# Five-stage language-model tower on one core: split float32 state-space products, expert blocks with the tokens as stationary operand, and register loads one pair ahead

## The chip, the cores and the metric

The kernel runs on one core of one Trainium2 chip. The time is what the device reports for one execution of the whole program, in microseconds (us). The median of three runs of the kernel before is 3116.32 us (3112.61 to 3125.64).

## The reference, cut to what matters

Eight sequences of 512 tokens, 256 channels each (x is 4096 x 256 in float32), pass through five stages, one after the other:

- **Tower**, four layers: `x = x + ssm(layernorm(x))`, then `x = x + gelu(layernorm(x) @ w1 + b1) @ w2 + b2`.
- Window attention, a stage that the change doesn't touch.
- **bfloat16 experts**: 8 experts, each token goes to its 2 best.
- Relative attention, not touched.
- **float32 experts**: 16 experts, the 2 best, beside a shared path.

The two formulas on which the change works:

```
# state-space part of a tower layer, for every sequence; H is a scan over the 512 tokens
u = x @ B                    # 256 -> 64 states
h = sigmoid(A) * h + u       # one step a token
y = H @ C + x @ D            # 64 -> 256 and 256 -> 256

# bfloat16 expert e, on the tokens that chose it
p1  = x @ mlp1[e].T + bias1[e]            # 256 -> 512, gate and linear part interleaved
act = g * sigmoid(1.702 g) * (lin + 1)    # g = min(p1 even, 7), lin = clip(p1 odd)
p2  = act @ mlp2[e].T + bias2[e]          # 256 -> 256
```

## The kernel before

All of x lies in SBUF from start to end. Each engine has a program of its own, written out by hand, and semaphores tie them together; there is no scheduler. A stage ends when all its engines have passed its last barrier.

**Tower (`tower_stage`).** 32 steps, one for a layer and a sequence. On TensorE, step j (`step`, L576) is: the first MLP product of sequence j, channels tile by tile (`mlp_in`, L557, in three parts of 4, 2 and 2 tiles); between these parts the two state-space products of the *next* step, `ssm_in(j + 1)` (L533) and `ssm_out(j + 1)` (L543 for D, L544 for C); the transposes of the normalised rows for the step after next (`turn1`, L132); the second MLP product (`mlp_out`, L571, four token tiles) with the transposes of the next step (`turn2`) between the second and the third tile. The MLP products take float32 data in two parts of type fp32r, a rounded high part and the rest, and sum three products, high x high, high x low and low x high (`TERMS`, L547); ScalarE makes the high part, VectorE the low one. The state-space products take plain float32; the profile shows two MATMUL rows for one such product, and one for a product in fp32r. ScalarE's step (L395) is 16 Gelu passes, `turn(j + 2)` (L371: two copies out of PSUM) and `turn2(j + 1)` (four copies, high and full). VectorE's step (L476) is, in this order: `norm1(j + 2)`, `low_hid` 0, `scan(j + 1)` (L430), `low_hid` 2 and 4, `add_y(j + 1)`, statistics of the second norm, `low_hid` 6, its application, `add_o` first half (L454), `low_xn2T(j + 1)` (L468), `add_o` second half. In the first step of a layer VectorE and ScalarE first split w2, in the last one they split the next w1. GpSimd gathers the embedding rows at the start (L172, 32 gathers), and computes the reciprocal roots.

**bfloat16 experts (`bf16_experts_stage`).** First, for each sequence b: norm, a second (mean square) norm, routing, and a scatter of the rows to DRAM, sorted by expert (8 indirect DMAs a sequence, L1172, from GpSimd). GpSimd's loop is, for b = 0 to 7: root of the first norm of b (`pool_rstd`, L117), root of the mean square of b (L1178), scatter of b - 2. VectorE can centre sequence b only when L117 is done. After the routing SyncE stores eight pad blocks (L1118), each at a row that it reads into a register, and only then loads blocks. Then 36 pairs of blocks of 128 rows go through a pipeline; in its iteration i TensorE does the transposes of pair i (L1495), the first product of pair i - 1 (L1508, with the bias L1509) and the second of pair i - 3 (L1520, L1523). The first product has the *weights* as stationary operand, 128 columns of them at an offset from a register, and 128 tokens as moving operand, 24 matrix instructions a pair; its result has the hidden channels on partitions, as the second product wants it. ScalarE's iteration is: copy of the transposes of i (L1243), Gelu of i - 1 (L1250), high part of i - 1 (L1257), copy of the result of i - 4 (L1264):

```
                    act.wait_ge(act_ready, j + 1)
                    if j >= 2:
                        act.wait_ge(y_done, j - 1)
                    act.activation(act_s[:, j % 2, 0, :, :, :], act_b[:, j % 2, :, :, :], ACT.Identity).then_inc(high_ready, 1)
```

Here j is i - 1, so that this copy waits until TensorE has finished the second product of pair i - 3, and the copy of the result of pair i - 4 stands behind it. GpSimd sends that result to DRAM with two indirect DMAs (L1186), and SyncE loads pair j into a ring of six buffers when pair j - 6 has been sent (L1127, L1128).

**float32 experts (`experts_stage`).** 39 pairs in a pipeline of the same kind: transposes of i (L2428), gate and up product of i - 1 (L2438), transposes of i - 2 (L2447), down product of i - 3 (L2455). The expert's offset is read into registers of TensorE between the transposes of i and the product of i - 1:

```
                    offset[j] = [pe.value_load(owner_at[0:1, 2 * j + s:2 * j + s + 1], min_val=0, max_val=(EX - 1) * WROW) for s in range(2)]
```

The bfloat16 stage has the same loads behind the first product, one pair ahead (`find`, L1481).

## Time and profile before

| | |
|---|---|
| runs, median (lowest to highest) | 3116.32 us (3112.61 to 3125.64) |
| profiled execution, its own time | 3127.48 us |
| its span, first to last instruction | 3125.8 us |
| TensorE busy, share of the span | 2495.2 us, 80% |
| VectorE busy | 1474.5 us, 47% |
| ScalarE busy | 1263.8 us, 40% |
| GpSimd busy | 691.0 us, 22% |
| mean granted TensorE clock | 0.845 of 2.4 GHz |

A busy time is the union of an engine's instructions, so that two that overlap count once. The granted clock is what the throttle gave TensorE: 1.00 stands for 2.4 GHz and 0.50 for 1.2 GHz. The profiled execution is 11.2 us above the median of the runs. By stage, roughly: the tower to 1190 us, window attention to 1423 us, the bfloat16 experts to 1937 us (preparation to 1590 us, the pairs to 1896 us), relative attention to about 2700 us, the float32 experts to the end (the pairs from 2905 to 3080 us).

### The profile page before, as it was taken

What the parts mean: (1) busy time and instruction counts of PE and PEld (TensorE: products, weight loads), DVE (VectorE), ACT (ScalarE), POOL (GpSimd) and SP (SyncE); (2) the same over time, 40 slices, a digit from 0 to 9 for tenths busy, and PEclk for the clock granted to TensorE, in tenths of its full rate; (3) what the DMA queues carried; (4) which work ended last, traced back from release to release, by engine and by line L of the source; (5) the groups of instructions that cost most, each with busy time, mean ns of one, the idle gap of its engine ahead of it and who ended that gap; (6) DMA issues with size and microseconds to landing.
All of it is one profiled execution on the core that took longest, in us unless ns stands there. A gap on an engine that the chain in (4) does not pass through costs nothing. (4 is left out here: it accounts for less than half of the span.)

```text
span 3125.8 us, 44495 instructions
## 1 busy us (share of the span) xinstructions
PE 2495.2 (80%) x13409; PEld 1759.7 (56%) x13409; DVE 1474.5 (47%) x4318; ACT 1263.8 (40%) x2520; POOL 691.0 (22%) x824
## 2 busy tenths in 40 slices
PE   2999999999999996982169991588988888695883
PEld 1777777777777774762135551255555555472662
DVE  3544554444454435634522225366666666460224
ACT  1434443444344432432312223376667667410221
POOL 4111111111111103203622222111121112226332
PEclk7999999999999998985555555699999999767987
DMA  9300100000000001222111114122222112222336
GB/s 217 41 1 5 30 1 0 13 23 1 5 3 1 0 1 36 41 49 62 39 44 49 48 49 140 47 67 65 63 62 63 59 41 66 55 62 90 102 118 217
DMA packets 202515, 162.18 MB, mean 52 GB/s; under 512 B 104945, under 2 KB 160673, under 8 KB 202337
## 3 DMA queue, kind: packets, MB, share of 16 engines
q1 hardware_dynamic: 184258, 118.51, 14.2%
q0 software_dynamic: 13856, 37.30, 4.0%
q10 hardware_dynamic: 4224, 4.19, 0.4%
q8 instruction: 88, 1.44, 0.2%
q14 instruction: 89, 0.73, 0.1%
HBM read 89.99 MB, written 69.95 MB: 51 GB/s over the span
## 5 line engine op out<-in xcount | busy, mean ns | idle before, releaser
L571 PE MATMUL psum_o<-w_s,hid_s 128*128 128x256 f32 x3072 | 384.2, 284 | 19.0 <-ACT hid L404 19.0
L557 PE MATMUL psum_h<-xn2T_s,w_s 128*128 128x512 f32 x1536 | 388.7, 402 | 5.4 <-ACT hid L404 3.3
L571 PEld LDWEIGHTS psum_o<-w_s,hid_s 128*128 128x128 f32 x3072 | 371.9, 188 | 26.9 <-issue 19.0
L403 ACT ACTIVATE hid_s<-psum_h,b 128x512 fp32r<-128x512 f32 x256 | 176.0, 688 | 435.1 <-PE psum_h L557 418.8
L557 PEld LDWEIGHTS psum_h<-xn2T_s,w_s 128*128 128x128 f32 x1536 | 277.3, 188 | 114.8 <-ACT hid L404 46.7
L1848 DVE CUSTOM_DVE_ANT_0 ra_z<-ra_psum_s,ra_rhat 128x128 f32<-128x128 f32 (+3 forms) x512 | 225.7, 482 | 230.5 <-PE ra_psum_s L1947 217.4
L1789 ACT ACTIVATE ra_p<-ra_z,ra_nm 128x128 f32<-128x128 f32 (+3 forms) x512 | 244.4, 555 | 0.0
L1959 PE MATMUL ra_psum_p<-ident,ra_p 128*128 128x128 f32 x1280 | 190.2, 302 | 62.5 <-POOL ra_p L1714 62.5
L1959 PEld LDWEIGHTS ra_psum_p<-ident,ra_p 128*128 128x128 f32 x1280 | 155.7, 153 | 98.0 <-issue 75.9
L1714 POOL TENSOR_SCALAR_AFFINE_SELECT ra_p<-ra_p 128x512 f32<-128x512 f32 x128 | 81.2, 634 | 556.4 <-DVE ra_p L1876 556.4
L1781 ACT ACTIVATE ra_pt<-ra_psum_p 128x1024 f32<-128x1024 f32 x128 | 131.0, 1024 | 166.5 <-PE ra_psum_p L1959 166.5
L473 DVE TENSOR_TENSOR hid_s<-hid,hid_s 128x1024 fp32r<-128x1024 f32 x128 | 155.5, 1215 | 84.3 <-ACT hid L404 84.0
L404 ACT ACTIVATE hid<-psum_h,b 128x512 f32<-128x512 f32 x256 | 174.0, 680 | 0.0
L1971 PE MATMUL ra_psum_o<-ra_pt,ra_v_now 128*32 128x512 f32 (+3 forms) x1024 | 171.5, 481 | 0.8 <-ACT ra_pt L1783 0.8
L1876 DVE TENSOR_SCALAR ra_p<-ra_p,ra_em 128x128 f32<-128x128 f32 (+3 forms) x512 | 162.6, 380 | 1.4 <-issue 1.4
L117 POOL TENSOR_TENSOR ln2n_rstd<-ln2n_var_eps,minus_half 128x4 f32<-128x4 f32 x32 | 32.3, 1008 | 525.7 <-DVE ln2n_var_eps L113 525.7
L543 PE MATMUL psum_y<-wd,xn1T 128*128 128x256 f32 x512 | 144.4, 405 | 2.0 <-DVE state L430 1.9
L1393 DVE TENSOR_SCALAR be_lin<-be_bank 128x512 f32<-128x512 f32 x36 | 24.9, 692 | 244.4 <-PE be_bank L1509 244.4
L379 ACT ACTIVATE xn2T_s<-psum_t,ln 128x512 fp32r<-128x512 f32 x64 | 46.4, 775 | 211.6 <-PE psum_t L132 211.6
L1947 PE MATMUL ra_psum_s<-ra_k_st,ra_q_st 48*128 48x128 f32 (+3 forms) x512 | 118.6, 352 | 15.0 <-DMA ra_k_st<-ra_scratch 14.5
L1186 POOL DMA_INDIRECT be_results<-be_ys,be_zs x72 | 69.0, 959 | 248.4 <-ACT be_ys L1264 236.5
L454 DVE TENSOR_TENSOR x<-psum_o,x 128x512 f32<-128x512 f32 (+1 forms) x64 | 44.3, 691 | 167.6 <-PE psum_o L571 167.6
(354 smaller groups left out, 4359.2 us busy)
## 6 DMA issues: line engine op xcount, KB each, us to landing
ex_slots<-blank SPq DMA_DIRECT2D x1, 10296.0 KB, 68.4
ex_zT<-ex_slots SPq DMA_DIRECT2D x39, 264.0 KB
ex_rows<-ex_slots SPq DMA_DIRECT2D x8, 1056.0 KB, 9.8
w<-in_L_tok_w SPq DMA_DIRECT2D x8, 1024.0 KB
be_rows<-be_results SPq DMA_DIRECT2D x8, 1024.0 KB, 5.3
ra_scratch<-ra_hi SPq DMA_DIRECT2D x32, 256.0 KB
ra_scratch<-ra_lo SPq DMA_DIRECT2D x32, 256.0 KB
ra_q_st<-ra_scratch SPq DMA_DIRECT2D x128, 64.0 KB, 1.8
```

The lines of the kernel that those rows point to most:

```text
L403: act.activation(hid_s[:, 0, m, :], psum_h[:, m % 2, :], ACT.Gelu, bias=b1[:, m:m + 1])
L404: act.activation(hid[:, m, :], psum_h[:, m % 2, :], ACT.Gelu, bias=b1[:, m:m + 1]).then_inc(hid_ready, 1)
L473: dve.tensor_tensor(hid_s[:, 1, m:m + 2, :], hid[:, m:m + 2, :], hid_s[:, 0, m:m + 2, :].bitcast(F32), ALU.subtract).then_inc(hid_lo, 1)
L543: pe.matmul(out, xn1T[:, parity, k, tok], wd[:, k, :], start=(k == 0), stop=False)
L557: mm = pe.matmul(psum_h[:, m % 2, :], w1_s[:, w_part, k, m * P:(m + 1) * P], xn2T_s[:, x_part, k, :], start=(n == 0 and k == 0), stop=(n = ...
L571: mm = pe.matmul(psum_o[:, t // 2, (t % 2) * D:(t % 2 + 1) * D], hid_s[:, h_part, m, t * P:(t + 1) * P], w2_s[:, w_part, m, :], start=(n = ...
L1781: act.activation(out[:, 0:8, :], psum_p[:, 0:2, :].rearrange("p c (a b) -> p (c a) b", a=4), ACT.Identity).then_inc(pt_act, 1)
L1789: act.activation(p[:, i % 2, t, 0:n], z[:, i % 2, t, 0:n], ACT.Exp, scale=SCALE, bias=nm[:, i % 2, t:t + 1]).then_inc(exp_done, 1)
L1848: dve.tensor_tensor_reduce(out=z[:, i % 2, t, 0:n], in0=scores[t], in1=rhat[:, i * T + T - n:(i + 1) * T], scale=1.0, scalar=0.0, op0=ALU. ...
L1876: last = dve.tensor_scalar(pt_, pt_, em[:, (i - 1) % 2, t:t + 1], None, ALU.max)
L1959: mm = pe.transpose(psum_p[:, c, a * P:(a + 1) * P], p[:, i % 2, q, k * P:(k + 1) * P], S.ident[:, :])
L1971: mm = pe.matmul(psum_o[u * HC:(u + 1) * HC, k * P:T], v_now[:, slot, k, :], pt[:, slot, first:first + n, :].rearrange("p a b -> p (a b)") ...
```

## The change

Tower: B, C and D are held in one tile `ssm` and split into two fp32r parts, as w1 and w2 are (`high_ssm` on ScalarE, `low_ssm` on VectorE, 1024 columns, once a layer, in the last step of the layer before). B is loaded twice side by side, and C twice, one copy below the other, so that the state appears on 128 partitions, twice the same 64 states. The normalised rows are split too: `turn` makes four copies in place of two, and `low_xn1T` is a new pass on VectorE, behind the application of the second norm. After the scan VectorE rounds the 128 rows of the state, and subtracts on the lower 64 rows, so that one product with K = 128 gives the high and the low part of the state times the high part of C, and a product with K = 64 adds the high part times the low part of C.

bfloat16 experts: the tokens become the stationary operand and 512 columns of weights the moving one, 6 matrix instructions a pair in place of 24; Gelu and clip run in two halves each, and the result is turned round with four float32 transposes into a PSUM bank, from which the high and the low part are made, one iteration later than before. The transposes of the rows have one PSUM buffer in place of two. GpSimd computes the root of the first norm one sequence ahead.

float32 experts: the register loads go behind the product, one pair ahead.

The diff, cut to its core:

```diff
-        wb = sb("wb", [P, DK, NS])
-        wc = sb("wc", [NS, D])
-        wd = sb("wd", [P, DK, D])
+        NP = 2 * NS
+        SSM_B, SSM_C, SSM_D = 0, DK * NP, DK * NP + D
+        SSM = SSM_D + DK * D
+        ssm, ssm_s = sb("ssm", [P, SSM]), sb("ssm_s", [P, 2, SSM], F32R)
...
-                (state_ready, NB * l, b_loaded, [(wb[:, :, :], mat("L0_tok_B")), (decay[:, :], decay_all[:, ds(l, 1)])]),
-                (y_done, NB * l, cd_loaded, [(wc[:, :], A["L0_tok_C"][ds(l, 1), :, :].rearrange("o s d -> (o s) d")),
-                                             (wd[:, :, :], mat("L0_tok_D"))]),
+                (ssm_split, l, ssm_loaded, ssm_pairs(l)),
+                (state_ready, NB * l, step_loaded, [(decay[:, :], decay_all[:, ds(l, 1)])]),
...
-                for k in range(DK):
-                    act.activation(xn1T[:, parity, k, :], psum_t[:, k, :], ACT.Identity,
-                                   scale=ln1[:, 0, k:k + 1], bias=ln1[:, 1, k:k + 1]).then_inc(xn1T_ready, 1)
+                if later(j):
+                    act.wait_ge(xn1T_lo, j)
+                for out, count in ((xn1T_s[:, parity, 0, :, :], 0), (xn1T[:, :, :], 1)):
+                    for k in range(DK):
+                        ins = act.activation(out[:, k, :], psum_t[:, k, :], ACT.Identity, scale=ln1[:, 0, k:k + 1], bias=ln1[:, 1, k:k + 1])
+                        if count:
+                            ins.then_inc(xn1T_ready, 1)
...
-                dve.tensor_tensor_scan(state[:, :], decay[:, 0:1].to_broadcast([NS, T]), psum_y[0:NS, 0, :],
+                dve.tensor_tensor_scan(state[:, :], decay[:, 0:1].to_broadcast([NP, T]), psum_y[0:NP, 0, :],
                                        0.0, ALU.mult, ALU.add).then_inc(state_ready, 1)
+                dve.wait_ge(state_ready, j + 1)
+                dve.tensor_copy(state_s[:, :], state[:, :]).then_inc(state_hi, 1)
+                dve.wait_ge(state_hi, j + 1)
+                dve.tensor_tensor(state_s[NS:NP, :], state[NS:NP, :], state_s[NS:NP, :].bitcast(F32), ALU.subtract).then_inc(state_split, 1)
...
+            def low_xn1T(j, parity):
+                dve.wait_ge(xn1T_ready, DK * (j + 1))
+                dve.tensor_tensor(xn1T_s[:, parity, 1, :, :], xn1T[:, :, :], xn1T_s[:, parity, 0, :, :].bitcast(F32),
+                                  ALU.subtract).then_inc(xn1T_lo, 1)
...
                     norm2_apply(j + 1)
-                if w1_of is not None:
-                    low_w1(w1_of)
+                if more2:
+                    low_xn1T(j + 2, parity)
+                if next_of is not None:
+                    low_w1(next_of)
...
-                for k in range(DK):
-                    mm = pe.matmul(psum_y[0:NS, 0, :], wb[:, k, :], xn1T[:, parity, k, :], start=(k == 0), stop=(k == DK - 1))
+                for n, (x_part, w_part) in enumerate(TERMS):
+                    for k in range(DK):
+                        mm = pe.matmul(psum_y[0:NP, 0, :], ssm_s[:, w_part, SSM_B + k * NP:SSM_B + (k + 1) * NP], xn1T_s[:, parity, x_part, k, :],
+                                       start=(n == 0 and k == 0), stop=(n == 2 and k == DK - 1))
...
-                    for k in range(DK):
-                        pe.matmul(out, xn1T[:, parity, k, tok], wd[:, k, :], start=(k == 0), stop=False)
-                    mm = pe.matmul(out, state[:, tok], wc[:, :], start=False, stop=True)
+                    for n, (x_part, w_part) in enumerate(TERMS):
+                        for k in range(DK):
+                            pe.matmul(out, xn1T_s[:, parity, x_part, k, tok], ssm_s[:, w_part, SSM_D + k * D:SSM_D + (k + 1) * D],
+                                      start=(n == 0 and k == 0), stop=False)
+                    if t == 0:
+                        pe.wait_ge(state_split, j + 1)
+                    pe.matmul(out, state_s[:, tok], ssm_s[:, 0, SSM_C:SSM_D], start=False, stop=False)
+                    mm = pe.matmul(out, state_s[0:NS, tok], ssm_s[0:NS, 1, SSM_C:SSM_D], start=False, stop=True)
...
+            nm[0].pool_rstd(pool, S.minus_half, 0)
             for b in range(NB):
-                nm[b % 2].pool_rstd(pool, S.minus_half, b // 2)
+                if b + 1 < NB:
+                    nm[(b + 1) % 2].pool_rstd(pool, S.minus_half, (b + 1) // 2)
...
-                    act.activation(gate[:, j % 2, :, :, :].rearrange("p s t n -> p (s t n)"), bank[2 + 2 * (j % 2)][:, :],
-                                   ACT.Gelu_apprx_sigmoid).then_inc(gated, 1)
-                if 0 <= i - 1 < PAIRS:
-                    j = i - 1
-                    act.wait_ge(act_ready, j + 1)
+                    for s in range(2):
+                        if s:
+                            act.wait_ge(lin_ready, 2 * j + 1)
+                        act.activation(gate[:, j % 2, s, :], bank[1 + 2 * (j % 2) + s][:, 0:I], ACT.Gelu_apprx_sigmoid).then_inc(gated, 1)
+                if 0 <= i - 2 < PAIRS:
+                    j = i - 2
+                    act.wait_ge(a_turned, j + 1)
                     if j >= 2:
                         act.wait_ge(y_done, j - 1)
-                    act.activation(act_s[:, j % 2, 0, :, :, :], act_b[:, j % 2, :, :, :], ACT.Identity).then_inc(high_ready, 1)
+                    act.activation(act_s[:, j % 2, 0, :], psum_a[:, :], ACT.Identity).then_inc(high_ready, 1)
...
                     for s in range(2):
-                        for it in range(IK):
-                            for half in range(2):
-                                to = bank[2 + 2 * (j % 2) + half][:, (s * IK + it) * P:(s * IK + it + 1) * P]
-                                at = (it * 2 + half) * P
-                                for k in range(DK):
-                                    pe.matmul(to, w1T[:, k, ds(offset[j][s] + at, P)], zsT[:, j % 2, s, k, :], start=(k == 0), stop=False)
-                                mm = pe.matmul(to, b1_row[0:2, ds(offset[j][s] + at, P)], ones2[0:2, :], start=False, stop=True)
+                        to = bank[1 + 2 * (j % 2) + s]
+                        for k in range(DK):
+                            pe.matmul(to[:, :], zsT[:, j % 2, s, k, :], w1T[:, k, ds(offset[j][s], WSTEP)], start=(k == 0), stop=False)
+                        mm = pe.matmul(to[:, :], ones2[:, :], b1_row[0:2, ds(offset[j][s], WSTEP)], start=False, stop=True)
                     mm.then_inc(p1_done, 1)
...
+                if 0 <= i - 2 < PAIRS:
+                    j = i - 2
+                    pe.wait_ge(act_ready, j + 1)
+                    if j:
+                        pe.wait_ge(low_ready, j)
+                    for s in range(2):
+                        for it in range(IK):
+                            at = (s * IK + it) * P
+                            mm = pe.transpose(psum_a[:, at:at + P], act_b[:, j % 2, s, it * P:(it + 1) * P], S.ident[:, :])
+                    mm.then_inc(a_turned, 1)
...
+            find(0)
             for i in range(PAIRS + 3):
...
-                    offset[j] = [pe.value_load(owner_at[0:1, 2 * j + s:2 * j + s + 1], min_val=0, max_val=(EX - 1) * WROW) for s in range(2)]
...
                     mm.then_inc(bgu_done, 1)
+                    if j + 1 < PAIRS:
+                        find(j + 1)
```

## Rows read from the trace of the kernel before

**Rows 1.** Windows: busy us (x instructions) of PE, PEld, DVE, ACT, POOL; clock, DMA.

```profile
80.00:1160.00 1080.00, 1055.86 (x5858) 823.21 (x5856) 524.16 (x1113) 461.73 (x703) 137.39 (x92) 1.00 0.05 9
...
1590.00:1896.00 306.00, 274.79 (x1368) 153.55 (x1368) 71.54 (x108) 82.61 (x145) 69.00 (x72) 0.50 0.16 48
...
2905.00:3080.00 175.00, 149.77 (x700) 121.12 (x701) 42.17 (x77) 49.38 (x117) 69.40 (x73) 0.90 0.36 108
```

**Rows 2.** Timeline, one tower step: start us, duration, engine, line.

```profile
660.65 5.99 PE L571 MATMUL psum_o<-w_s,hid_s 128*128 128x256 f32 x48
...
663.87 1.23 DVE L468 TENSOR_TENSOR xn2T_s<-xn2T,xn2T_s 128x1024 fp32r<-128x1024 f32 x1 [3.12 <-ACT xn2T L379]
...
666.48 5.99 PE L557 MATMUL psum_h<-xn2T_s,w_s 128*128 128x512 f32 x24
...
672.39 1.93 PE L533 MATMUL psum_y<-xn1T,wb 128*64 128x512 f32 x4
...
674.51 1.21 DVE L430 TENSOR_TENSOR_SCAN state<-decay,psum_y 64x512 f32<-64x512 f32 x1 [1.13 <-PE psum_y L533]
...
677.16 1.03 PE L543 MATMUL psum_y<-wd,xn1T 128*128 128x256 f32 x4
...
683.81 3.06 PE L557 MATMUL psum_h<-xn2T_s,w_s 128*128 128x512 f32 x12
...
688.06 1.45 ACT L371 ACTIVATE xn1T<-psum_t,ln 128x512 f32<-128x512 f32 x2
```

**Rows 3.** Timeline, PE alone: the start of the tower step after that.

```profile
700.78 5.98 PE L557 MATMUL psum_h<-xn2T_s,w_s 128*128 128x512 f32 x24
```

**Rows 4.** Timeline, the first step of a layer: its start and its scan.

```profile
354.30 2.95 PE L557 MATMUL psum_h<-xn2T_s,w_s 128*128 128x512 f32 x12
...
364.44 1.21 DVE L430 TENSOR_TENSOR_SCAN state<-decay,psum_y 64x512 f32<-64x512 f32 x1
```

**Rows 5.** Timeline, start of the tower: an embedding add, transposes at the low clock.

```profile
54.78 1.23 DVE L197 TENSOR_TENSOR x<-x,pos 128x1024 f32<-128x1024 f32 x1 [5.39 <-DMA x<-in_L_tok_emb,idx]
...
62.20 1.97 PE L132 MATMUL psum_t<-ident,xn 128*128 128x128 f32 x8 [19.39 <-DVE xn L123]
```

**Rows 6.** Timeline, POOL alone, bfloat16 experts, one sequence of the preparation.

```profile
1510.66 1.04 POOL L117 TENSOR_TENSOR be_n_rstd<-be_n_var_eps,minus_half 128x4 f32<-128x4 f32 x1
1515.20 1.01 POOL L1178 TENSOR_TENSOR be_rms<-be_ms_eps,minus_half 128x4 f32<-128x4 f32 x1 [3.50 <-DVE be_ms_eps L1297]
...
1526.50 1.04 POOL L117 TENSOR_TENSOR be_n_rstd<-be_n_var_eps,minus_half 128x4 f32<-128x4 f32 x1
```

**Rows 7.** Timeline, SP's queue, bfloat16 experts: the pad blocks.

```profile
1563.59 22.27 SPq L1118 DMA_DIRECT2D be_slots<-be_pads  x8
```

**Rows 8.** Timeline, bfloat16 experts, two iterations of the pairs.

```profile
1643.05 0.61 PE L1495 MATMUL be_bank<-be_ident,be_zs 128*128 128x128 bf16 x4 [1.32 <-DMA be_zs<-be_slots]
...
1647.66 0.42 PE L1520 MATMUL be_bank<-be_b_row,be_ones 1*128 x1
...
1650.57 0.60 PE L1495 MATMUL be_bank<-be_ident,be_zs 128*128 128x128 bf16 x4
1650.80 0.63 ACT L1257 ACTIVATE be_act_s<-be_w_raw 128x512 fp32r<-128x512 f32 x1 [2.30 <-PE be_bank L1523]
...
1651.34 0.58 ACT L1264 ACTIVATE be_ys<-be_bank 128x512 f32<-128x512 f32 x1
...
1659.85 0.61 PE L1495 MATMUL be_bank<-be_ident,be_zs 128*128 128x128 bf16 x4 [1.48 <-DMA be_zs<-be_slots]
```

**Rows 9.** Timeline, float32 experts: an iteration after a DMA wait, and the next.

```profile
2998.86 0.66 PE L2428 MATMUL ex_bank<-ident,ex_zT 128*128 128x128 f32 x4 [1.30 <-DMA ex_zT<-ex_slots]
...
3000.40 3.51 PE L2438 MATMUL ex_bank<-ex_w,ex_zT 128*128 x8 [0.89 <-ACT ex_zT L2173]
...
3005.27 1.89 PE L2438 MATMUL ex_bank<-ex_w,ex_zT 128*128 x8
```

**Rows 10.** Waits, same pairs: us in total, times, longest us.

```profile
PE ex_bank L2438 <- ACT ex_zT L2173: 11.4, 13, 1.0
```

More of the change, by code:

```diff
@@ L274, in mat, with ssm_pairs @@
                 return A[name][ds(l, 1), :, :].rearrange("o (k p) n -> p (o k) n", p=P)
+            def ssm_pairs(l):
+                b_twice = ssm[:, SSM_B:SSM_C].rearrange("p (k u n) -> p k u n", k=DK, u=2)
+                return ([(b_twice[:, :, u, :], mat("L0_tok_B")) for u in range(2)]
+                        + [(ssm[u * NS:(u + 1) * NS, SSM_C:SSM_D], A["L0_tok_C"][ds(l, 1), :, :].rearrange("o s d -> (o s) d")) for u in range(2)]
+                        + [(ssm[:, SSM_D:SSM].rearrange("p (k n) -> p k n", k=DK), mat("L0_tok_D"))])
             return [
@@ L297, in layer @@
                 step(l * NB + NB - 2, 0, True, not last)
-                step(l * NB + NB - 1, 1, not last, not last, w1_of=None if last else l + 1)
+                step(l * NB + NB - 1, 1, not last, not last, next_of=None if last else l + 1)
             layer(0, False)
@@ L308, in _ @@
         def _(sp):
-            sp.dma_start(decay_in[:, :], A["L0_tok_A_diag"].rearrange("l s -> s l")).then_inc(decay_loaded, 16)
+            for u in range(2):
+                sp.dma_start(decay_in[u * NS:(u + 1) * NS, :], A["L0_tok_A_diag"].rearrange("l s -> s l")).then_inc(decay_loaded, 16)
             embedding.sync_loads(sp)
@@ L312, in _ @@
             w1_first, w2_first = first[0], first[1]
-            ln1_first, b_first, cd_first, ln2_first, b1_first, b2_first = first[2:]
+            ln1_first, ssm_first, step_first, ln2_first, b1_first, b2_first = first[2:]
             sp.wait_ge(decay_ready, 1)
-            for _, _, arrived, pairs in [ln1_first, b_first, cd_first, ln2_first, w1_first, b1_first, w2_first, b2_first]:
+            for _, _, arrived, pairs in [ln1_first, ssm_first, step_first, ln2_first, w1_first, b1_first, w2_first, b2_first]:
                 for to, frm in pairs:
@@ L381, in turn2, with high_ssm @@
                             ins.then_inc(xn2T_ready, 1)
+            def high_ssm(l):
+                act.wait_ge(ssm_loaded, 80 * (l + 1))
+                if later(l):
+                    act.wait_ge(y_done, NB * l)
+                act.activation(ssm_s[:, 0, :], ssm[:, :], ACT.Identity).then_inc(ssm_hi, 1)
             def high_w1(l):
@@ L406, in step @@
                     turn(j + 2, parity)
-                if w1_of is not None:
-                    high_w1(w1_of)
+                if next_of is not None:
+                    high_w1(next_of)
                 if more:
                     turn2(j + 1)
+            high_ssm(0)
             high_w1(0)
@@ L474, in low_hid, with step @@
                                   ALU.subtract).then_inc(hid_lo, 1)
-            def step(j, parity, more, more2, w2_of=None, w1_of=None):
+            def step(j, parity, more, more2, w2_of=None, next_of=None):
                 if w2_of is not None:
                     low_w2(w2_of)
+                if next_of is not None:
+                    low_ssm(next_of)
                 if more2:
@@ L505, in _ @@
             embedding.vector_embed(dve, 1)
+            low_ssm(0)
+            low_xn1T(0, 0)
             scan(0)
@@ L514, in _ @@
             norm1(1)
+            low_xn1T(1, 1)
             for b in range(NB - 2, NB):
@@ L574, in mlp_out, with step @@
                     mm.then_inc(o_done, 1)
-            def step(j, parity, more, more2, w2_of=None, w1_of=None):
+            def step(j, parity, more, more2, w2_of=None, next_of=None):
                 mlp_in(j, range(FM // 2))
@@ L1048, in bf16_experts_stage @@
         zsT = sb("zsT", [P, 2, 2, DK, P], BF16)
-        lin = sb("lin", [P, 2, 2, IK, P])
+        lin = sb("lin", [P, 2, 2, I])
         early = w1_raw[:, :, :].rearrange("p r h -> p (r h)").bitcast(F32)
-        gate, act_b = (early[:, n * 4 * IK * P:(n + 1) * 4 * IK * P].rearrange("p (u s t n) -> p u s t n", u=2, s=2, t=IK) for n in range(2))
-        act_s = sb("act_s", [P, 2, 2, 2, IK, P], F32R)
-        square = lin[:, :, :, :, :].rearrange("p u s t n -> p (u s t n)").rearrange("p (t n) -> p t n", t=TT)
+        gate, act_b = (early[:, n * 4 * I:(n + 1) * 4 * I].rearrange("p (u s n) -> p u s n", u=2, s=2) for n in range(2))
+        act_s = sb("act_s", [P, 2, 2, T], F32R)
+        square = lin[:, :, :, :].rearrange("p u s n -> p (u s) n")
         ys = sb("ys", [P, YRING, 2, D])
@@ L2420, in _, with find @@
             offset = {}
+            def find(j):
+                offset[j] = [pe.value_load(owner_at[0:1, 2 * j + s:2 * j + s + 1], min_val=0, max_val=(EX - 1) * WROW) for s in range(2)]
+            find(0)
             for i in range(PAIRS + 3):
```

81 lines of the change are left out of this document (42 added, 39 removed).

## The prediction

> **What bounds the kernel now.** I read the windows by stage first, then the timeline inside each stage that the change touches. In the tower TensorE is busy 1056 of 1080 us at a granted clock of 1.00 [rows 1]: matrix work bounds it, and the other engines are half idle. The timeline of a step shows the same, one product against the next, with a period of 700.78 - 666.48 = 34.3 us [rows 2, 3]. In the bfloat16 pairs TensorE is busy 275 of 306 us, at 0.50 of the clock [rows 1], but two iterations of them begin with a DMA wait, and what they wait for is a ring: load, three iterations, copy of the result, scatter, next load [rows 8]. In the float32 pairs the same holds in every third iteration or so [rows 9]. In the preparation of the bfloat16 experts GpSimd's order of work sets the pace, at 1526.50 - 1510.66 = 15.8 us a sequence [rows 6].
>
> **Tower, the products.** A product of 512 columns in fp32r costs 3.06 / 12 = 0.255 us, one of 256 columns 5.99 / 48 = 0.125 us [rows 2]. `ssm_in` goes from 1.9 us (four rows of plain float32, two for each product) to 6 x 0.255 = 1.5. `ssm_out` takes 683.81 - 677.16 = 6.65 us now; it becomes 4 tiles x 8 products x 0.125 = 4.0. That is 0.4 + 2.65 = 3.05 us a step, all of it on TensorE's path.
>
> **Tower, what is added.** ScalarE's `turn` grows by 1.45 us, the price of its present two copies [rows 2]. It runs under `mlp_out` 0 and 1, which last 6 us and must have its result at their end; it would be done some 3 us earlier. The cost is nothing; without that cover it would be 1.45 us a step. `low_xn1T` is a pass like L468, 1.23 us [rows 2], behind the norm and before `add_o`, where VectorE waits for TensorE: nothing. The weights' split is once a layer about 1 us on ScalarE and 1.23 on VectorE, in the last step, where the scan waited 1.13 us for TensorE [rows 2] and the next wait has slack: nothing. The five loads on SyncE's queue in place of three or four come a step and more ahead.
>
> The serial part is the state. The scan now has two passes behind it, a rounding and a subtraction, before the C products of the first tile. The trace shows no such rounding. Its bounds are 0.4 (a third of a 1024-column pass) and 1.23 us [rows 2]; I take 0.7 for each of the two, nearest to half of the 1024 columns plus a fixed part. The scan starts at 674.51, 0.35 earlier afterwards, and ends 1.21 later; with two hand-overs the split is there at 677.0. TensorE reaches `ssm_out` at 676.8 and has six D products (0.75 us) that don't need it: it wants the split at 677.5. So the new wait is hidden by half a microsecond. At 1.23 us each it would come 0.5 us late, 16 us in 31 steps. What is queued behind these passes on VectorE are `low_hid` 2 and 4, whose Gelus come later anyway.
>
> In the first step of a layer VectorE has split w2 before, and the scan comes 364.44 - 354.30 = 10.1 us into the step, against 8.0 in the other [rows 2, 4]. There the split comes about 1.3 us late: 4 x 1.3 = 5 us. At the start of the program the longer chain (two more copies, two more VectorE passes) lies under the embedding gathers, which VectorE still awaits at 54.78 [rows 5]; but in step 0 `low_xn1T(1)` stands ahead of the last embeddings, and I give that step no gain. Tower: 30 x 3.05 - 5 = **-87 us**.
>
> **Preparation of the bfloat16 experts.** GpSimd's cycle is root (1.04), 3.50 us idle until the mean square is there, root (1.01), then eight scatters to 1526.50 [rows 6]. The idle time exists because VectorE centres a sequence only after the first root. With the root a sequence ahead, the centring falls under the scatters and the idle time goes; it stands in five of the eight cycles, so 17 us. What ends next are the scatters themselves, 10 us a sequence. The pad blocks on SyncE's queue (22.27 us, [rows 7]) hang on the last routing and move with it: **-17 us**, between -5 (the routing chain takes the idle time) and -18.
>
> **bfloat16 pairs.** An iteration of TensorE is 1650.57 - 1643.05 = 7.52 us: 4.61 for the transposes and the first product, 2.91 for the second [rows 8]. The copy of the result starts 0.77 us after that, because ScalarE's high copy waits for the second product (2.30 us idle, L1257) and the result stands behind it. From this copy at 1651.34 it is 8.51 us to the transposes of the pair two iterations later, at 1659.85 [rows 8]. Two iterations are thus 7.52 + 0.77 + 8.51 = 16.8 us, 8.4 a pair: the ring is the bound, not TensorE alone.
>
> Afterwards, at 1.2 GHz, the first product is six instructions of 512 columns, 0.43 us each (512 / 1.2 GHz; above, twice the 0.255 of [rows 2], 0.51). With 0.4 for the transposes of the rows, 4 x 1.97 / 8 = 1.0 for the new float32 transposes [rows 5] and 2.9 for the second product that makes 6.9 us (up to 7.4). The ring changes too. The high copy is an iteration later and no longer waits for the second product, so the result is copied about 4.8 us into the iteration rather than 8.3; two iterations need 4.8 + 8.51 = 13.3, 6.7 a pair. TensorE's 6.9 becomes the bound, the ring close behind. 36 x (8.4 - 6.9) = **-54 us**; at 7.4, -36. That the rows' transposes share one PSUM buffer costs nothing, as their copy is done during the second product. ScalarE has about 2.8 us of copies in 6.9.
>
> **float32 pairs.** After a DMA wait the product stands 0.89 us behind the transposes, while the registers load (the row puts it down to the copy of the transposes, which that product doesn't need) [rows 9]; 13 such waits make 11.4 us [rows 10]. Then the eight matrix instructions take 3.51 us instead of 1.89 [rows 9], as the clock has fallen in the gap. With the loads ahead the gap goes, as it did in the bfloat16 stage. It lies on the ring, so its time is won, unless the load is merely awaited longer. I take the 11 us and a third of the lost clock: **-15 us**, between 0 and -25.
>
> **The sum.** 87 + 17 + 54 + 15 = 173 us. The profiled execution took 3127.5 us, so 2954; the median of the runs is 11 us lower, and I give **2942 us** against 3116.
>
> **The rivals.**
>
> *The ring does not shorten.* If the copy of the result still comes late in the iteration, two iterations need 16 us, and the pairs win 12 rather than 54; if the float32 gap too is only exchanged for a longer DMA wait, another 12 go. About 2990 us. For it: both rings wait for DMA now. Against it: the present lateness has its cause in the row of L1257. Chance 0.14.
>
> *The products are not cheaper*: the shapes with the state behave otherwise than the MLP's, say half the gain is gone. 2985 us, chance 0.04.
>
> *Slower than before.* The place is the wait on `state_split` in `ssm_out`: if it lets TensorE stand for 2 us a step, the clock falls as in [rows 9], and the following products run at half speed. A step's 31 us of products would become some 57. It decides from 173 / 26 = 7 such steps; with 10 of them, 2942 + 260 = 3200 us. Against it: clock 1.00 over 1080 us [rows 1], no such gap in a step [rows 2], and even the dear bound makes a wait of 0.5 us. Chance 0.01.
>
> **How the numbers follow.** The forecast has 0.55, the clock 0.25, the ring 0.14, the products 0.04, slower 0.01, anything near no change 0.01. About 0.5% can be told from no change in this kernel. The forecast's own bounds are the dear state passes (+16), 7.4 us a pair (+18), the preparation (+12) and the float32 pairs (+15 or -10); not all together. The range of 2890 to 2990 us takes in the clock case and most of the ring case. Faster 0.98, same 0.01, slower 0.01.
>
> **What would show it.** Right: a tower period of 31.2 us, `ssm_out` at 4.0; 12.3 us a sequence in the preparation; 6.9 us a pair with ScalarE's L1264 before the second product's end; no wait between L2428 and L2438. Wrong: a wait of PE for DVE's state passes in every step; a clock well over 0.50 in the pairs; SyncE waiting for scatters with pairs of 8 us; a step period that stays at 33 or 34 us.

## The result, and the profile after it

The changed kernel takes 3009.68 us (median; 2993.97 to 3018.84) beside 3119.11 us for the kernel of before on the same chip: 0.964 of its time, 95% interval 0.960 to 0.969. Faster, as forecast, but by 109 us where 174 were forecast, and above the range of 2890 to 2990 us.

The stages follow one another, so each one's length can be read from the last VectorE instruction of each. All times in us; the chip of the second pair is another one, where both kernels run some 25 us or more faster:

| stage | before | after | difference | forecast | second pair |
|---|---|---|---|---|---|
| tower | 1173.8 | 1124.8 | -49.0 | -87 | 1173.2, 1121.7 |
| window attention | 249.2 | 251.8 | +2.6 | 0 | 248.6, 250.8 |
| bfloat16 experts | 512.7 | 443.4 | -69.3 | -71 | 507.5, 434.6 |
| relative attention | 784.4 | 803.9 | +19.5 | 0 | 780.4, 800.7 |
| float32 experts | 405.8 | 392.5 | -13.3 | -15 | 375.4, 361.6 |
| span | 3125.8 | 3016.2 | -109.6 | -173 | 3085.1, 2969.5 |

So two of three changed stages came out within 2 us, the tower gave 38 us less than forecast, and a stage whose code is the same in both kernels lost 20. A difference of a stage between two executions is not all due to an edit: the bfloat16 experts of the changed kernel took 443.4 and 434.6 us here, and 428.3 and 422.7 in two kernels below whose edits touch neither their preparation nor their pairs. In windows, the profile after, with the columns of [rows 1] (tower; preparation and pairs of the bfloat16 experts; relative attention; pairs of the float32 experts):

```profile
80.00:1110.00 1030.00, 1001.35 (x6182) 867.06 (x6181) 612.79 (x1211) 508.94 (x769) 158.47 (x92) 0.99 0.05 10
...
1376.00:1528.00 152.00, 23.12 (x243) 18.76 (x244) 77.64 (x382) 44.11 (x110) 92.42 (x100) 0.51 0.19 60
1528.00:1756.00 228.00, 198.22 (x782) 101.20 (x796) 74.16 (x135) 81.99 (x168) 59.45 (x62) 0.69 0.19 57
1820.00:2624.00 804.00, 646.11 (x3584) 399.85 (x3584) 483.14 (x1972) 503.60 (x1060) 150.13 (x315) 0.87 0.18 54
...
2818.00:2962.00 144.00, 126.24 (x659) 102.81 (x659) 38.83 (x71) 47.00 (x111) 65.38 (x68) 0.99 0.42 127
```

The tower is as dense as before. In the bfloat16 pairs the clock is no longer 0.50 but 0.69 on average. Relative attention had the same 3584 matrix instructions in the kernel before:

```profile
1936.00:2720.00 784.00, 630.87 (x3584) 393.53 (x3584) 484.22 (x1972) 502.22 (x1060) 149.69 (x315) 0.89 0.19 56
```

The timeline of one tower step after the change, as [rows 2]:

```profile
642.75 1.23 DVE L503 TENSOR_TENSOR xn2T_s<-xn2T,xn2T_s 128x1024 fp32r<-128x1024 f32 x1 [3.12 <-ACT xn2T L392]
...
645.36 5.97 PE L605 MATMUL psum_h<-xn2T_s,w_s 128*128 128x512 f32 x24
...
651.16 1.56 PE L578 MATMUL psum_y<-xn1T_s,ssm_s 128*128 128x512 f32 x6
...
652.91 1.22 DVE L452 TENSOR_TENSOR_SCAN state<-decay,psum_y 128x512 f32<-128x512 f32 x1 [0.65 <-PE psum_y L578]
...
654.16 0.43 DVE L455 CAST state_s<-state 128x512 fp32r<-128x512 f32 x1
654.62 0.69 DVE L457 TENSOR_TENSOR state_s<-state,state_s 64x512 fp32r<-64x512 f32 x1
...
655.36 0.88 PE L589 MATMUL psum_y<-ssm_s,xn1T_s 128*128 128x256 f32 x6
...
656.08 0.28 PE L593 MATMUL psum_y<-ssm_s,state_s 128*128 128x256 f32 x1
656.29 0.18 PEld L594 LDWEIGHTS psum_y<-ssm_s,state_s 64*128 64x128 f32 x1
656.29 0.38 PE L594 MATMUL psum_y<-ssm_s,state_s 64*128 64x256 f32 x1
656.60 0.77 PEld L589 LDWEIGHTS psum_y<-ssm_s,xn1T_s 128*128 128x128 f32 x6
...
660.60 3.06 PE L605 MATMUL psum_h<-xn2T_s,w_s 128*128 128x512 f32 x12
```

The state is split at 655.3, and TensorE needs it at 656.08: it doesn't wait. The period, from L503 to L503 of the next step, is 674.85 - 642.75 = 32.1 us (median of all steps 32.2, before 34.3); 31.2 was forecast. `ssm_out` lasts 660.60 - 655.36 = 5.24 us, not 4.0. Look at the last product of an output tile, L594: its weight load (engine PEld, which brings the stationary operand into the array) starts at the same moment as its matrix instruction, while the load of L593 starts 0.12 us ahead of its own. A tile thus costs 656.60 - 655.36 = 1.24 us, and 1.33 where such a product stands ahead of it too, and not eight times 0.125.

### The profile page after: what moved, and what is told of

Its sections match the earlier page's. It is cut to its first block and busy times, and to the rows that moved or that the text cites. A ratio compares the mean times of both kernels' runs of the same rounds, so it can differ in the third digit from the quotient of the medians.

```text
span 3016.2 us, 43729 instructions
## 1 busy us (share of the span) xinstructions
PE 2376.3 (79%) x13211; PEld 1756.8 (58%) x13225; DVE 1572.0 (52%) x4454; ACT 1319.7 (44%) x2624; POOL 716.0 (24%) x824
## 5 line engine op out<-in xcount | busy, mean ns | idle before, releaser
L605 PEld LDWEIGHTS psum_h<-xn2T_s,w_s 128*128 128x128 f32 x1536 | 284.6, 191 | 90.4 <-ACT hid L425 21.5
L2028 PE MATMUL ra_psum_o<-ra_pt,ra_v_now 128*32 128x512 f32 (+3 forms) x1024 | 182.5, 505 | 0.8 <-ACT ra_pt L1840 0.8
L2028 PEld LDWEIGHTS ra_psum_o<-ra_pt,ra_v_now 128*32 128x32 f32 x1024 | 59.9, 123 | 121.3 <-issue 108.6
L589 PE MATMUL psum_y<-ssm_s,xn1T_s 128*128 128x256 f32 x768 | 124.8, 299 | 3.0 <-DVE state L452 3.0
L1444 DVE TENSOR_SCALAR be_lin<-be_bank 128x256 f32<-128x256 f32 x72 | 30.3, 425 | 174.9 <-PE be_bank L1555 162.7
L345 POOL TENSOR_TENSOR x<-x,b 128x1024 f32 (+1 forms) x32 | 99.0, 3093 | 79.5 <-DVE xn L123 68.7
```

Of the source, the lines that this page charges most:

```text
L589: pe.matmul(out, xn1T_s[:, parity, x_part, k, tok], ssm_s[:, w_part, SSM_D + k * D:SSM_D + (k + 1) * D], start=(n == 0 and k == 0), stop=F ...
L605: mm = pe.matmul(psum_h[:, m % 2, :], w1_s[:, w_part, k, m * P:(m + 1) * P], xn2T_s[:, x_part, k, :], start=(n == 0 and k == 0), stop=(n = ...
L2028: mm = pe.matmul(psum_o[u * HC:(u + 1) * HC, k * P:T], v_now[:, slot, k, :], pt[:, slot, first:first + n, :].rearrange("p a b -> p (a b)") ...
```

## The experiments

Each kernel below is compared with runs of the kernel before on its own chip (medians 3091 to 3096 us; 3128 for the two parts undone).

**The same two kernels again.** No edit.

> The kernel of before, unchanged. Question: is the relative attention stage (identical code in both kernels; 784.4 us before at a granted clock of 0.93 in its middle, 803.9 us after at 0.89) longer in the changed kernel because of the change, or does it vary from one execution to the next? If it varies: anything between 784 and 805 us here, and the float32 experts' preparation (185.1 us before, 194.0 after) varies too. If the stage's length belongs to the kernel: 784 us within 1, and 185 us.

> The changed kernel, unchanged. If the length of the relative attention stage varies by execution: somewhere between 784 and 805 us. If it belongs to the kernel (for instance by where the stage's instructions lie): 804 us within 1. The tower's period stays at 32.2 us and the stall of 4.8 us in front of the first product of layer 2 stands again if it is a stall of the program's, not of one execution.

Measured: 780.4 and 800.7 us in relative attention. Both are 3 to 4 us below the lengths that were asked for, but the difference of 20 us is there again: it belongs to the kernel, though the stage's code is the same. The float32 preparation took 163.9 and 163.8 us here, against 185.1 and 194.0 in the first pair, so its difference of 9 us there does not come from the change. The stall ahead of the first product of layer 2, which the waits put down to "issue", is 3.1 us here, 4.8 in the first profile of the changed kernel and 1.8 in that of before.

**All 128 rows of the split state.**

```diff
-                    mm = pe.matmul(out, state_s[0:NS, tok], ssm_s[0:NS, 1, SSM_C:SSM_D], start=False, stop=True)
+                    mm = pe.matmul(out, state_s[:, tok], ssm_s[:, 1, SSM_C:SSM_D], start=False, stop=True)
```

> The changed kernel with the low part of C multiplied with all 128 rows of the split state (high and low) rather than with its upper 64. The sum gains the term low x low, which the other products leave out; the number of instructions stays. Theory: a product with 64 rows between products with 128 shows its weight load in the open, once going in and once coming out, and that is the 0.33 us by which an output tile (1.33 us) is dearer than eight products of 0.125. Then a tile takes 1.00 us, the step 32.2 - 1.3 = 30.9 us, the tower 40 us less, the kernel about 2970 us. Rival: the two products with the state cost more whatever their rows (their operand comes from VectorE's tile): the tile stays at 1.33 us and nothing changes.

Measured: 2916.73 us, 0.944 of the kernel before (0.941 to 0.947); tower 1075.4 us after 1121.7; step 30.7 us. Beside the one run of the changed kernel on this chip (2972.08 us) that is 55 us less; the tower's 46 are the edit's, the rest lies in the bfloat16 experts and in relative attention, 6 us each, where nothing was edited. The timeline of a tile in this kernel:

```profile
660.80 0.88 PE L589 MATMUL psum_y<-ssm_s,xn1T_s 128*128 128x256 f32 x6
661.41 0.19 PEld L593 LDWEIGHTS psum_y<-ssm_s,state_s 128*128 128x128 f32 x1
661.52 0.28 PE L593 MATMUL psum_y<-ssm_s,state_s 128*128 128x256 f32 x1
661.53 0.19 PEld L594 LDWEIGHTS psum_y<-ssm_s,state_s 128*128 128x128 f32 x1
661.64 0.28 PE L594 MATMUL psum_y<-ssm_s,state_s 128*128 128x256 f32 x1
...
661.76 0.40 PE L605 MATMUL psum_h<-xn2T_s,w_s 128*128 128x512 f32 x1
```

Every load is again 0.11 us ahead of its product, and the tile takes 661.76 - 660.80 = 0.96 us. The array has more work, and the product is cheaper: its number of rows, not its operand, made the difference. The profile of before shows the same mark, in its timeline of a tile:

```profile
678.12 0.29 PEld L544 LDWEIGHTS psum_y<-wc,state 64*128 64x128 f32 x2 [0.33 <-issue]
678.12 0.70 PE L544 MATMUL psum_y<-wc,state 64*128 64x256 f32 x2
...
678.74 0.30 PEld L543 LDWEIGHTS psum_y<-wd,xn1T 128*128 128x128 f32 x2 [0.33 <-issue]
```

The loader stands idle for 0.33 us going into the product with 64 rows and again coming out of it. In all three kernels a load is not pulled ahead across a change from 128 to 64 rows or back. The Trainium skill (TensorE: Matmul & The Clock Gate, Part 2: What happens when you issue a matmul) says that a weight load is pulled ahead of running products when the row groups don't conflict or when it goes to the background weights; which of the two fails here, no run shows.

**Ten buffers in place of six.** In both rings of blocks (in the bfloat16 ring the four more buffers lie in memory that the preparation has done with, and SyncE waits for its end before the first load; the diff is cut to its core):

```diff
-        RING, YRING = 6, 4
+        RING, YRING = 10, 4
```

> The changed kernel with ten buffers in place of six in the ring of blocks, in the bfloat16 and in the float32 pairs. Theory: TensorE's waits for loads (19 waits, 22 us without the first, in the bfloat16 pairs; 17 waits, 17.5 us, in the float32 pairs) are the ring, and each wait also helps to close the clock (0.69 in the bfloat16 pairs). Then the waits go, bfloat16 pairs fall from 6.53 us to between 5.0 and 5.9 us each (22 to 54 us less), float32 pairs from 3.91 to between 3.3 and 3.5 us (15 to 22 us less). Rival: the loads are late because SyncE or GpSimd issue them late, not because a buffer is missing: then the waits stay where they are, and both stages keep their times within 5 us.

> The kernel of before with ten buffers in place of six in both rings. It separates what the ring and what TensorE's work bring: the changed kernel with ten buffers took 4.31 us a bfloat16 pair at a clock of 0.91. Theory of the prediction: the ring bounds the pairs of the kernel before (8.4 us in the steady part, 7.98 over all), so without it TensorE's 7.5 us at 0.50 of the clock are left; 36 x 0.5 to 0.9 makes 15 to 30 us less. Rival: the waits were what kept the clock at 0.50; without them it opens and the pairs take 4 to 5.5 us, 90 us or more less. Float32 pairs: 4.13 to 4.33 us fall to 3.3 to 3.9 (the register loads still stand behind the transposes).

Measured: the changed kernel with it 2862.67 us, 0.926 of before (0.923 to 0.929); the kernel before with it 3024.74 us, 0.978 (0.975 to 0.981). The pairs' windows, first of the changed kernel, then of the kernel before, each with ten buffers:

```profile
1515.00:1666.00 151.00, 149.30 (x802) 79.55 (x799) 72.17 (x135) 79.69 (x169) 58.03 (x61) 0.91 0.28 86
```

```profile
1585.00:1837.00 252.00, 250.33 (x1280) 142.77 (x1279) 66.83 (x101) 74.70 (x134) 57.57 (x60) 0.50 0.17 52
```

Per bfloat16 pair: 8.0 us before, 7.2 with ten buffers, 6.5 after the change, 4.3 after it with ten buffers. For the changed kernel 5.0 to 5.9 had been expected, so the gain was undervalued. The waits for loads were the ring's. And the clock: the old layout stays at 0.50 even when TensorE is busy 250.33 of 252 us, so the waits had not held it down. In the new layout, with the tokens as stationary operand and 512 columns in a stream, it stands at 0.91, and with six buffers at 0.69. The new layout differs in more than the length of the stream (a fourth of the instructions, four float32 transposes more), and which of it opens the clock was not tried. The waits of TensorE in the pairs, six buffers and then ten:

```profile
PE be_bank L1544 <- DMA be_zs<-be_slots: 20.3, 17, 3.9
```

```profile
PE be_bank L1547 <- DMA be_zs<-be_slots: 1.7, 1, 1.7
```

The 17 waits hold 20 us; the other 58 of the 78 us that four buffers bring come with the clock, 0.91 in place of 0.69. The Trainium skill (TensorE: Matmul & The Clock Gate, Part 1: The HAM clock gate) says that the clock follows how busy TensorE has been. By the busy share that the profile gives, 99% at 0.50, the old layout does not bear that out; that share is modelled from pipelined instructions, and what the clock follows in its place no run shows.

In the float32 pairs the register loads hardly count once the ring is long: 3.21 us a pair with the old place, 3.17 with the new. Both lie just below what had been expected (3.3 to 3.9 and 3.3 to 3.5).

**The copy of the result first.** The kernel of before, two blocks of ScalarE's iteration exchanged:

```diff
+                if 0 <= i - 4:
+                    j = i - 4
+                    act.wait_ge(y_done, j + 1)
...
                 if 0 <= i - 1 < PAIRS:
                     j = i - 1
                     act.wait_ge(act_ready, j + 1)
...
-                if 0 <= i - 4:
-                    j = i - 4
-                    act.wait_ge(y_done, j + 1)
...
```

> The kernel of before with one thing moved: ScalarE copies the result of pair i - 4 ahead of the high part of pair i - 1. Theory of the prediction: the copy of the result stood behind a wait for the second product, this lengthened the ring, and the ring bounded the pairs. Then the copy comes some 3 us earlier in the iteration, two iterations of 16.8 us fall towards twice TensorE's 7.5, and the stage is 15 to 30 us shorter. Rival: only TensorE's fewer and longer matrix instructions made the pairs faster; then the stage keeps its time within 5 us.

Measured: 3059.05 us, 0.989 (0.986 to 0.991). The stage takes 476.9 us after 507.5, a pair 7.2 us after 8.0, as much as with ten buffers. The timeline of ScalarE, where L1258 is now the copy of the result and L1264 the high part:

```profile
1647.50 0.59 ACT L1258 ACTIVATE be_ys<-be_bank 128x512 f32<-128x512 f32 x1
1649.90 0.63 ACT L1264 ACTIVATE be_act_s<-be_w_raw 128x512 fp32r<-128x512 f32 x1 [1.81 <-PE be_bank L1523]
```

TensorE's waits for the ring in the pairs, in the kernel of before and in this one:

```profile
PE be_bank L1495 <- DMA be_zs<-be_slots: 23.4, 17, 2.1
```

```profile
PE be_bank L1495 <- DMA be_zs<-be_slots: 1.1, 3, 0.4
```

So in the kernel of before the late copy was what lengthened the ring beyond TensorE's work; the prediction read that rightly.

**VectorE's standstills moved.** Why is relative attention longer? Laid side by side instruction by instruction, the two kernels differ there first on VectorE: between the statistics of the norm and their aggregate. The timeline of VectorE in the fourth sequence, before and after:

```profile
2178.63 0.38 DVE L110 BATCH_NORM_AGGREGATE ra_n_mv<-ra_n_stats 128x2 f32<-128x6 f32 x4 [0.15 <-DVE ra_n_stats L106]
```

```profile
2066.00 0.38 DVE L110 BATCH_NORM_AGGREGATE ra_n_mv<-ra_n_stats 128x2 f32<-128x6 f32 x4 [0.52 <-DVE ra_n_stats L106]
```

It is 0.15 us in all eight sequences before and 0.52 from the third on after. The kernel of before has a like gap, of 0.31 us, 63 records further on in the same loop, and the changed kernel has one more 129 records behind its first. The change puts 63 more instructions of VectorE's program ahead of this stage (a loop's body counted once). So these look like places in the program, 128 instructions apart, where VectorE stands still whatever instruction lies there. To try it, VectorE gets instructions that wait for a semaphore long reached, in the drain of the bfloat16 stage, where it idles. Two such waits make one instruction, so that 130 are 65, and 126 in the other kernel 63:

```diff
             low(PAIRS - 1)
+            for _ in range(130):
+                dve.wait_ge(share_ready, NB)
             dve.wait_ge(share_ready, NB)
```

> The changed kernel with 65 more instructions that only wait for a semaphore long reached, on VectorE, between the end of the bfloat16 pairs and the sum of the results (VectorE idles there). Theory: VectorE stands still for 0.31 to 0.37 us each time it passes certain places of its program, 128 instructions apart; the change put 63 instructions ahead of the relative attention stage, so that such a place fell between the statistics and their aggregate (0.52 us in place of 0.15 in every sequence), the transposes behind it came later, and the clock dipped more (stage 800 us in place of 784). With 65 more the places fall as in the kernel before: the gap at the aggregate 0.15 us again, the stage 780 to 785 us, the kernel 15 us less. Rival: the stage is longer for another reason (ScalarE's or TensorE's program, or the clock alone): 795 to 804 us as now.

> The kernel of before with 63 such instructions at the same place. Theory: the gap in front of the aggregate goes from 0.15 to 0.52 us in the sequences 2 to 7 and the relative attention stage from 780 to 784 us to between 793 and 804. Rival, as above: nothing moves.

Measured, the same row first in the changed kernel with 65 more, then in the kernel before with 63 more:

```profile
2036.78 0.38 DVE L110 BATCH_NORM_AGGREGATE ra_n_mv<-ra_n_stats 128x2 f32<-128x6 f32 x4 [0.15 <-DVE ra_n_stats L106]
```

```profile
2175.24 0.38 DVE L110 BATCH_NORM_AGGREGATE ra_n_mv<-ra_n_stats 128x2 f32<-128x6 f32 x4 [0.52 <-DVE ra_n_stats L106]
```

Relative attention takes 781.6 us with 65 more and 796.8 with 63 more: the stall changed sides, and the time with it. All twelve kept profiles agree: six with 0.15 us at the aggregate took 780 to 785 us for the stage, six with 0.52 took 795 to 804. The kernel before became slower by 0.6% (1.006, 1.004 to 1.008) through instructions that do nothing; the changed one stands at 0.955 (0.953 to 0.958) on a chip on which it was not itself run. A stall of 0.37 us per sequence cannot make 15 to 20 us by itself. The timeline of TensorE in the third sequence shows what goes with it, first before, then after, the transposes of the normalised rows and the output products:

```profile
2095.37 0.66 PE L1907 MATMUL ra_psum_w<-ident,ra_xn 128*128 128x128 f32 x4 [0.44 <-DVE ra_xn L123]
...
2101.63 2.70 PE L1971 MATMUL ra_psum_o<-ra_pt,ra_v_now 128*32 128x512 f32 x16
```

```profile
1978.59 0.66 PE L1964 MATMUL ra_psum_w<-ident,ra_xn 128*128 128x128 f32 x4 [0.81 <-DVE ra_xn L123]
...
1984.84 4.25 PE L2028 MATMUL ra_psum_o<-ra_pt,ra_v_now 128*32 128x512 f32 x16
```

The transposes are awaited 0.37 us longer, and the same 16 products take 4.25 us at a granted clock of 0.55 where they took 2.70 at 0.86. Between the aggregates of the fourth and the fifth sequence (2178.63 to 2267.56 before, 2066.00 to 2159.70 after) it takes 93.7 us in place of 88.9. That the later transposes make the clock open later is read from these rows; no run tried it apart. The window of the stage with 65 more:

```profile
1793.00:2575.00 782.00, 624.21 (x3584) 388.40 (x3584) 483.87 (x1973) 502.74 (x1060) 149.75 (x315) 0.90 0.19 56
```

The clock is 0.90 as against 0.87, TensorE's busy time 624 us as against 646 for the same instructions.

**Two parts undone.** In the changed kernel, `pool_rstd` of sequence b back at the head of its turn, and the register loads of the float32 pairs back between the transposes and the product:

```diff
-            nm[0].pool_rstd(pool, S.minus_half, 0)
             for b in range(NB):
-                if b + 1 < NB:
-                    nm[(b + 1) % 2].pool_rstd(pool, S.minus_half, (b + 1) // 2)
+                nm[b % 2].pool_rstd(pool, S.minus_half, b // 2)
...
-            find(0)
...
+                    find(j)
...
-                    if j + 1 < PAIRS:
-                        find(j + 1)
```

> The changed kernel with two parts undone: in the bfloat16 preparation GpSimd computes the root of the first norm of sequence b at the head of its own turn again, and in the float32 pairs TensorE loads the registers of pair i - 1 between the transposes and the product again. Theory of the prediction: the preparation goes back from 142.6 us to about 160 (a cycle of 15.8 us in place of 12.3), the float32 pairs from 3.79 to between 4.1 and 4.3 us each (12 to 20 us over the 38), the kernel about 30 us slower than the changed one. Rival: these gains came from elsewhere (the loads of the pads, the clock): preparation below 150 us, float32 pairs at 3.8.

Measured: 3041.65 us, 0.971 of before (0.968 to 0.974), against 0.964 for the changed kernel: some 21 us back, where 30 had been expected. This chip is like that of the first pair, and there the stages compare: preparation of the bfloat16 experts 167.5 us (151.5 after the change, 167.8 before), float32 pairs 4.03 us (3.80 and 4.33). The root's place is the whole gain of the preparation. In the float32 pairs the wait behind the transposes is back (the name in the row is the one that [rows 10] has for it):

```profile
PE ex_bank L2497 <- ACT ex_zT L2228: 16.3, 19, 1.0
```

By the first pair of profiles the loads account for 0.23 of 0.53 us. But the kernel of before took 4.33 us a pair there and 4.06 to 4.13 in the profiles from other chips, the changed one 3.79 to 3.89 throughout. So the loads are between 0.14 and 0.24 us a pair, 5 to 9 us in all, and whether a rest is left cannot be told from the spread of the kernel before.

**The three edits at once.**

> The changed kernel with the three edits at once: low part of C against all 128 rows, rings of ten, 65 more waiting instructions on VectorE. Each alone took off the changed kernel, by stage: tower 46 us (1121.7 to 1075.4), bfloat16 experts 85 us (434.6 to 349.3), relative attention 19 us (800.7 to 781.6), float32 experts 23 us (361.6 to 338.3). The stages follow one another, so if the places where VectorE stands still fall as before they add to 173 us: about 2972 - 173 = 2800 us, ratio to before 0.905. Rival: the clock of a stage hangs on how the stage before left it, or the places fall otherwise, and a part of it is lost: 2815 to 2830 us.

Measured: 2793.81 us (2791.20 to 2801.41), 0.903 of before (0.901 to 0.904), as the sum of the stages said: it beats both kernels by far. Tower 1075.8, bfloat16 experts 350.9, relative attention 784.5, float32 experts 338.8 us.

## Why the prediction was right or wrong

**Tower, the products: wrong by a term of the sum.** "`ssm_out` ... it becomes 4 tiles x 8 products x 0.125 = 4.0" took every product for equal. The product with 64 rows costs its own 0.12 us and (5.24 - 3.84) / 4 = 0.35 more, since its weight load and the next one stand open: 5.24 us instead of 4.0, and 3.84 with 128 rows. `ssm_in` was 1.4 us for 1.5 forecast. The period fell by 2.1 us, not 3.05, and over 30 steps that is 29 of the 38 us that are missing. The rows that said it were in the timeline of before, on the loader's line, which the prediction did not read: its prices are those of the MLP products, which all have 128 rows.

**Tower, what is added: right, but for the start.** The rounding took 0.43 us and the subtraction 0.69 (0.7 forecast for each); TensorE waited for the split twice, 0.4 us in all. The first step of a layer came about 1.2 us later (1.3 forecast). Wrong was the start: "the longer chain ... lies under the embedding gathers", but the first L503 stands at 71.1 us, its like before (L468) at 67.0, and the first step took 1.9 us more. A second load of the decays is queued on SyncE's queue ahead of the token ids, so that the first gather starts at 5.98 us after 5.25; with more loads beside it the first embedding is there at 19.56 after 17.33, and GpSimd's root, behind which the next gathers stand, moves with it. The last gather is issued 4.1 us later, as much as L503; that the loads cause it is read from these rows, and no run moved one. And one transition between layers, where TensorE waits for nothing that the profile shows, cost 3 us more in the first pair of profiles (4.8 after 1.8).

**Preparation: right.** Its cycle on GpSimd:

```profile
1457.54 1.04 POOL L117 TENSOR_TENSOR be_n_rstd<-be_n_var_eps,minus_half 128x4 f32<-128x4 f32 x1
...
1469.87 1.04 POOL L117 TENSOR_TENSOR be_n_rstd<-be_n_var_eps,minus_half 128x4 f32<-128x4 f32 x1
```

That is 12.3 us as forecast, and 16.3 us were won of 17.

**bfloat16 pairs: the right sum by luck, from three wrong parts.** 54 us were forecast and about 52 came. But the 8.4 us a pair of before was read from two iterations, and over all pairs it was 7.98: with 6.9 after it the forecast would have been 39 us. At the low clock an iteration takes 7.3 us, not 6.9. And the clock does not stay low; the timeline of TensorE in two iterations:

```profile
1649.04 0.65 PE L1544 MATMUL be_bank<-be_ident,be_zs 128*128 128x128 bf16 x4
1649.49 1.06 PE L1554 MATMUL be_bank<-be_w1T,be_zsT 128*128 x2
...
1656.38 0.65 PE L1544 MATMUL be_bank<-be_ident,be_zs 128*128 128x128 bf16 x4
...
1660.59 0.74 PE L1580 MATMUL be_bank<-be_w2T,be_act_s 128*128 x4
1662.31 0.40 PE L1544 MATMUL be_bank<-be_ident,be_zs 128*128 128x128 bf16 x4 [0.97 <-DMA be_zs<-be_slots]
```

First 7.34 us at 0.50; then, from 1658 us on, the clock is 1.00, the work ends at about 1661.2, and the ring makes TensorE wait; from 1664 to 1666 us the clock is 0.61 and behind that 0.50 again. So the rival "the clock opens" was half true, with the counter-argument that the prediction itself gave: "the waits that then open would close the clock again". Its chance of 0.25 was too low, and the likeliest case should have been this mixture. That the ring would become the bound at 5.7 us was nearly right as well: the iteration at the open clock that ends with the ring's wait takes 1662.31 - 1656.38 = 5.93 us.

**float32 pairs: right in size, for the stage in part by chance.** 15 us were forecast. The pairs gave 20 us on the first chip and 13 on the second; the stage's 13.3 on the first holds 9 us that the preparation lost, which do not come from the change. No wait stands any more between transposes and product, and the clock is 0.99.

**Relative attention: not in the sum at all.** The prediction took stages with unchanged code for unchanged time, a term put at nothing without a reason. That cost 19.5 us of the 68 that the median lies above the forecast. Of the rest, window attention's 2.6 us (2.2 in the second pair) were not explained; VectorE's places moved there too, which was not tried.

With the tower's 38 us and these 22 the working is off by 60 of 63.4 us in the profiled executions. The first goes the way of the rival "the products are not cheaper", to which the prediction gave 0.04, though a third of the products' gain went (0.95 of 3.05 us a step) and not half; the second stood nowhere.

## What to carry to other kernels

Read the weight loads' line beside the matrix instructions' line: a product with fewer rows than its neighbours was dear on both sides here, and filling its rows with something useful or harmless was cheaper than leaving them out. When a wait for a ring goes away, look at what the clock does next: here four more buffers were worth 78 us, of which the waits themselves were 20. And a stage whose code is unchanged can still move, because an edit shifts where the rest of the program lies; compare such stages before you credit or blame an edit, and keep 1% of the time for it.

## What the runs showed of the hardware

VectorE stood still for 0.31 to 0.37 us at places of its program 128 instructions apart, at every pass of the loop of relative attention (some 460 instructions); they stayed where they were when the program shifted beneath them. That a semaphore wait in an idle stretch can win or lose 15 to 20 us in a stage of 780 was not expected. TensorE's clock did not follow the profile's busy share: 0.50 at 99% in the layout with 128-column products, 0.91 at 99% in the one with 512-column ones. A weight load was not pulled ahead across a change in the number of rows; the products of the two bias rows in the bfloat16 pairs show the same mark (0.32 us each with ten buffers at the full clock, beside about 0.26 for the products ahead of them).
